# A routed feed-forward kernel: first layer's weights folded, fp16 halves made before the scatter, engine loops unrolled

## The chip, the cores and the metric

One core of one Trainium2 chip runs the whole kernel. The metric is the device time of one execution in microseconds (us). The engines are TensorE (PE), VectorE (DVE), ScalarE (ACT), GpSimd (POOL) and SyncE (SP); each has a queue of its own that runs in order, and they meet in semaphores.

## The reference

The input is x of 16 x 256 rows of 128 numbers (4096 tokens). Two steps are computed, each followed by a LayerNorm of the sum with its input:

1. An attention-like step. Differences of neighbouring rows are normed, compared with 64 guidance vectors (a softmax over dot products), blended with them, and summed over a window of the last eight positions with fixed weights.
2. A feed-forward step with eight experts. Each token goes to the one expert with the largest router probability, and that probability is its gate:

```python
xn = (xt - mu) * rsqrt(var + LN_EPS) * ln_g + ln_b
h = relu(xn @ W1[expert] + b1[expert])      # 128 -> 512
y = (h @ W2[expert] + b2[expert]) * gate    # 512 -> 128
out = layernorm(xt + y)
```

All arrays are float32, and W1 and W2 hold 2 MB each.

## The kernel before, in words

**Windows.** The 4096 tokens are cut into 8 units of 4 tiles of 128. A software pipeline written out in Python runs over turns i; in each turn an engine does the steps of several units. SyncE first issues all loads in one queue: x in pieces, the constants, W1 behind the second piece, the rest of x, then the small ones (Wr, br, ln_g, ln_b; semaphore `small`), W2, and the biases. In turn i VectorE does `window(i)` (mixing of unit i-1, LayerNorm statistics of unit i-2, routing of units i-3 and i-4), `diff(i+2)`, `factors(i)`, in turns 2 to 4 some maxima of W2, and then `directions(i+1)`, which gives the normed rows N; in turns 0 and 1 two maxima of W1 each stand behind that. TensorE does `nT_(i)` (transposes of N), `logits(i-3)`, `sims(i)` (one fp32 matmul of 512 columns), `traj(i-1)`, `rank(i-3)`, `infl(i)`, `xT_(i-2)`. ScalarE copies `nT_`, exponentiates `et`, does `tanh`, `x1` (the first LayerNorm's output), `sumsq`, `xT_` and `np_`, in that order. GpSimd takes the roots (`mag_roots`, `std_roots`) and, in turn i, scatters unit i-4 to DRAM: four indirect DMAs of 128 rows each (L374), each token to the region of its expert, so that afterwards every block of 128 rows belongs to one expert. A row is `ROW = D + 4` floats: x1, the gate's part, the root of the second LayerNorm, and the token number.

**Weights.** For layer matmuls at fp16 speed with nearly fp32 precision, each operand is split in a high and a low fp16 half, and three products are summed. `scales` finds powers of two, `weights_hi` (ScalarE) and `split_lo` (VectorE) make the halves, in turns 7 and later; the last two `split_lo` stand behind the block table. The biases are split in three bf16 parts (`split_bias`), and a matmul with a selector (`sel16`) adds them.

**Blocks.** There are NB = 39 blocks, each of which loads its 128 rows (`XR`), and whose expert is read from a table into registers. Per block: ScalarE scales the rows (`b_xs`, L668), TensorE transposes them in fp32 (L518), ScalarE applies scale and bias per channel (`b_xt`, L673) and makes the high half (`b_xh`, L677), VectorE the low half (`b_xl`, L1000). Layer one is 4 chunks of 4 matmuls (`b_h`: bias L545, then L547, L548, L549). ScalarE makes the relu's high half (`b_hh`, L682), VectorE the low one (`b_hl`, L1006). Layer two (`b_y`) is 4 matmuls of 256 columns (L559: high by both weight halves, into two parts of a PSUM bank), 4 of 128 (L562) and a bias (L561). VectorE adds the two parts to x1 with the gate (`b_z0` L1011, `b_z` L1015), takes statistics, and ScalarE writes `OUT`. GpSimd computes the gate (`token`: cg L398, tok L399) and stores the block by an indirect DMA (`store`, L405). `steps` runs these with fixed leads; the first and last blocks are written out, and between them an engine loop takes eight blocks per turn.

## Time and profile before

| | us |
|---|---|
| Median of 3 runs | 222.06 (220.68 to 222.31) |
| Profiled execution, first to last instruction (span) | 219.4 |
| TensorE busy | 151.0 (69%) |
| VectorE busy | 171.0 (78%) |
| ScalarE busy | 141.9 (65%) |
| GpSimd busy | 122.4 (56%) |

Of the profiled execution only the span is given; a run's time lies 2.7 us above it by the median. Busy time is the sum of an engine's instructions; a matmul counts with its pipeline, so neighbours overlap, and starts tell more than durations. The windows end with the last scatter shortly before 120 us; the blocks take the rest. "Granted clock" is the share of full speed that TensorE was given.

### The profile page before, as it was taken

How to read it: one execution, taken by the hardware profiler on the slowest of the kernel's cores; microseconds unless marked ns; L12 is line 12 of the kernel's file. 1: busy time of each engine (PE TensorE's matmuls, PEld its weight loads, DVE VectorE, ACT ScalarE, POOL GpSimd, SP SyncE). 2: the span in 40 equal slices, each digit the busy share in tenths (PEclk: the TensorE clock that was granted, in tenths of full speed). 3: DMA queues.
4: the chain of work that ended last, by engine and by line, in shares of the span. 5: the costliest groups of instructions: out<-in, count | busy, mean ns of one | idle time of the engine just before them, and what ended most of it. 6: DMA issues, size and time to landing. Idle time of an engine off the chain costs nothing.

```text
span 219.4 us, 5683 instructions
## 1 busy us (share of the span) xinstructions
PE 151.0 (69%) x1395; PEld 125.6 (57%) x1396; DVE 171.0 (78%) x792; ACT 141.9 (65%) x425; POOL 122.4 (56%) x210
## 2 busy tenths in 40 slices
PE   0158975989785989662500199979979979979600
PEld 0014854776664768552400089869869869868500
DVE  2538789878889889986779139989979979989910
ACT  2455619473817386658502288979979979989530
POOL 4322233325728676687777220667767767768670
PEclk9999997585968596655555559999999999999955
DMA  5996760000101010100133211222221221220000
GB/s 154 334 366 190 224 185 0 3 1 0 51 0 38 17 37 14 51 25 25 37 93 106 75 37 28 65 62 56 71 73 52 64 73 54 70 62 23 30 9 0
DMA packets 16409, 15.66 MB, mean 71 GB/s; under 512 B 2810, under 2 KB 13142, under 8 KB 16386
## 3 DMA queue, kind: packets, MB, share of 16 engines
q1 hardware_dynamic: 13458, 10.83, 17.4%
q0 software_dynamic: 2272, 4.27, 5.9%
q10 hardware_dynamic: 656, 0.30, 0.5%
q8 instruction: 9, 0.15, 0.3%
q14 instruction: 14, 0.11, 0.2%
HBM read 10.52 MB, written 5.33 MB: 72 GB/s over the span
## 4 chain that ended last, share of the span: by engine, by line
PE 37%; POOL 18%; issue 13%; DVE 12%; ACT 8%; DMA 5%; DVEq 2%; SPq 1%; ACTq 1%; POOLq 1%
POOL rows L374 12%; PE bank L559 7%; PE bank L545 4%; PE bank L547 4%; PE bank L549 4%; PE bank L548 4%; PE bank L562 3%; PE bank L450 3%; DMA XN<-in_attn_embeddings 3%; PE bank L471 3%; PE bank L518 2%; POOL rstd L362 2%; POOL R L366 2%; ACT sq L578 2%; DVE hl L1006 2%
## 5 line engine op out<-in xcount | busy, mean ns | idle before, releaser
L405 POOL DMA_INDIRECT out<-OUT,tok x39 | 40.5, 1038 | 29.3 <-issue 29.0
L374 POOL DMA_INDIRECT rows<-R,place x32 | 33.9, 1061 | 9.0 <-issue 9.0
L545 PE MATMUL bank<-sel,bias 96*128 (+1 forms) x156 | 35.2, 225 | 5.2 <-issue 5.2
L547 PE MATMUL bank<-xh,W1h 128*128 128x128 f16 x156 | 35.0, 225 | 0.0
L549 PE MATMUL bank<-xh,W1l 128*128 128x128 f16 x156 | 34.8, 223 | 0.0
L548 PE MATMUL bank<-xl,W1h 128*128 128x128 f16 x156 | 34.7, 222 | 0.0
L559 PE MATMUL bank<-W2hl,hh 128*128 x156 | 32.7, 274 | 0.9 <-DVE hl L1006 0.8
L1006 DVE SCALAR_TENSOR_TENSOR hl<-bank,hh 128x512 f16<-128x512 f32 x39 | 26.6, 682 | 6.5 <-ACT hh L682 6.4
L450 PEld LDWEIGHTS bank<-V,C 128*128 128x128 f32 x128 | 24.9, 299 | 11.2 <-issue 11.2
L450 PE MATMUL bank<-V,C 128*128 128x129 f32 x128 | 26.8, 393 | 3.0 <-DVE Y L772 3.0
L562 PE MATMUL bank<-W2hl,hl 128*128 x156 | 28.0, 219 | 0.0
L682 ACT ACTIVATE hh<-bank 128x512 f16<-128x512 f32 x39 | 23.3, 597 | 6.6 <-PE bank L549 6.5
L518 PE MATMUL bank<-C,xs 128*128 128x128 f32 x39 | 11.9, 304 | 14.0 <-ACT xs L668 14.0
L691 ACT ACTIVATE OUT<-z,sd 128x128 f32<-128x128 f32 x39 | 19.4, 499 | 2.5 <-DVE sd L1033 2.5
L668 ACT ACTIVATE xs<-XR 128x128 f32<-128x128 f32 x39 | 15.7, 404 | 7.7 <-DMA XR<-rows 7.6
L362 POOL TENSOR_TENSOR rstd<-var_in,minus_half 128x4 f32<-128x4 f32 x8 | 8.2, 1020 | 20.1 <-DVE var_in L803 20.1
L545 PEld LDWEIGHTS bank<-sel,bias 96*128 96x128 bf16 x156 | 15.5, 99 | 6.4 <-issue 6.0
L559 PEld LDWEIGHTS bank<-W2hl,hh 128*128 128x128 f16 x156 | 15.2, 97 | 5.5 <-issue 2.9
L673 ACT ACTIVATE xt<-bank,gbs 128x128 f32<-128x128 f32 x39 | 17.9, 458 | 0.1
L1000 DVE TENSOR_TENSOR xl<-xt,xh 128x128 f16<-128x128 f32 x39 | 12.4, 318 | 6.0 <-ACT xh L677 6.0
L471 PE MATMUL bank<-nT,gdT 128*64 128x512 f32 x16 | 13.1, 912 | 5.0 <-ACT nT L599 5.0
L547 PEld LDWEIGHTS bank<-xh,W1h 128*128 x156 | 15.7, 100 | 0.6
(162 smaller groups left out, 448.8 us busy)
## 6 DMA issues: line engine op xcount, KB each, us to landing
XR<-rows SPq DMA_DIRECT2D x39, 66.0 KB, 1.8
W<-in_ffn_W SPq DMA_DIRECT2D x1, 2048.0 KB, 11.5
X<-in_attn_embeddings SPq DMA_DIRECT2D x2, 512.0 KB, 9.0
X<-in_attn_embeddings SPq DMA_DIRECT2D x1, 768.0 KB
out<-OUT,tok POOLq DMA_INDIRECT x39, 2.3
XN<-in_attn_embeddings SPq DMA_DIRECT2D x2, 256.0 KB, 8.3
rows<-R,place POOLq DMA_INDIRECT x32, 2.4
C<-in_constants SPq DMA_DIRECT2D x1, 428.0 KB, 4.6
```

Source lines behind the costliest of these rows:

```text
L374: pool.indirect_dma_start(out=rows[:, :], out_offset=bass.IndirectOffsetOnAxis(ap=place[u % 4][:, k:k + 1], axis=0), in_=R[u % 4][:, k, :] ...
L405: pool.indirect_dma_start(out=out[:, :], out_offset=bass.IndirectOffsetOnAxis(ap=tok[k][:, 0:1], axis=0), in_=OUT[k][:, :], in_offset=None ...
L450: m = pe.matmul(tile_of(traj_ps, k), band[a][k % 2], V[u % 3][:, 2 * (k // 2) + a, :], start=a == 0, stop=a == 1)
L471: pe.matmul(sims_ps[0:G, :], gdT[:, :], nT[:, :], start=True, stop=True).then_inc(s["sims_ps"], 1)
L545: pe.matmul(h, bias3[:, c * P:(c + 1) * P], sel, start=True, stop=False)
L547: pe.matmul(h, wh, xh[k][:, :], start=False, stop=False)
L548: pe.matmul(h, wh, xl[k][:, :], start=False, stop=False)
L549: m = pe.matmul(h, wl, xh[k][:, :], start=False, stop=True)
L559: pe.matmul(y[:, 0:2 * D], hh[k][:, c * P:(c + 1) * P], w, start=c == 0, stop=False)
L562: m = pe.matmul(y[:, 0:D], hl[k][:, c * P:(c + 1) * P], W2hl[:, bass.ds(e * FC + c, 1), 0:D], start=False, stop=c == FC - 1)
L682: act.activation(hh[k][:, :], bank[1 + k % 4][:, :], ACT.Relu).then_inc(every["hh"], 1)
L1006: stt(hl[k][:, :], bank[1 + k % 4][:, :], 0.0, hh[k][:, :], ALU.max, ALU.subtract).then_inc(t["hl"][k], 1)
```

## The change

It does the following.

- The second LayerNorm's gain and offset and b1 go into W1. With s = 4 the rows become s (xhat + 1), and since xhat sums to zero, each expert's W1 becomes ln_g W1 + c, with one c per column, (sum of (ln_b - ln_g) W1, plus b1) / 128. TensorE computes c by two fp32 matmuls of 512 columns per expert (`fold`, two experts in each of turns 1 to 4, in banks 0 and 1), with stationaries that VectorE prepares in turn 0 (`stationary`); VectorE applies it (`fold`). The bias matmuls of layer one go. W1's halves wait for the fold.
- The scaled row and its fp16 halves are made in the windows (`xs_`, `xh_` on ScalarE, `rest` on VectorE) and scattered with x1; a row is now 2 D + 8 = 264 floats. In a block two fp16 transposes and one ScalarE copy replace xs, transpose, xt, xh and xl.
- Layer two accumulates all in 128 columns of one bank: 13 matmuls, and one VectorE instruction for z.
- The engine loops are written out; row buffers are 16 rather than 8, and GpSimd scatters the output by the token number in the row buffer, without tok.
- The biases in three parts are b2 only; b1 is loaded by itself behind ln_b.

The diff, cut to its core:

```diff
-ROW = D + 4
+ROW = 2 * D + 8
+X1 = D
+GATE = 2 * D
+TOKEN = 2 * D + 1
+SIGMA = 4.0
 UN = 8
+RN = 16
...
+            sp.dma_start(b1[:, :], b1_in).then_inc(ld["b1"], 16)
             sp.dma_start(W2[:, :, :, :], w2.rearrange("e (c p) d -> p e c d", p=P)).then_inc(ld["w2"], 16)
             sp.wait_ge(s["zeroed"], 1)
             for j in range(3):
-                sp.dma_start(bias[32 * j:32 * j + E, 0:FF], b1).then_inc(ld["bias"], 16)
-                sp.dma_start(bias[32 * j:32 * j + E, FF:FF + D], b2).then_inc(ld["bias"], 16)
...
+                n = j % RN
+                if j >= RN:
+                    sp.wait_ge(every["xT_ps"], j - RN + 1)
+                    sp.wait_ge(every["z"], j - RN + 1)
+                    sp.wait_ge(every["cg"], j - RN + 1)
+                    sp.wait_ge(stored[n], 16 * (j // RN))
+                sp.dma_start(XR[n][:, :], rows[bass.ds(row[k], P), :]).then_inc(row_loaded[n], 16)
+            for n in range(RN):
+                sp.wait_ge(stored[n], 16 * (NB // RN + (n < NB % RN)))
...
                 pool.wait_ge(s["var2_in"], u + 1)
+                if u >= 2:
+                    pool.wait_ge(s["xs"], u - 1)
+                pool.tensor_tensor(r2[u % 2][:, :], var_in[u % 2][:, 1, :], half[:, :], ALU.pow).then_inc(s["r2"], 1)
                 if u >= 4:
                     pool.wait_ge(scattered[u % 4], 16 * NT * (u // 4))
-                pool.tensor_tensor(R[u % 4][:, :, D + 1], var_in[u % 2][:, 1, :], half[:, :], ALU.pow)
-                pool.tensor_copy(R[u % 4][:, :, D + 2].bitcast(I32), C[:, C_TOK + u * NT:C_TOK + (u + 1) * NT]).then_inc(s["r2"], 1)
...
-                pool.wait_ge(s["r2"], u + 1)
+                pool.wait_ge(s["token"], u + 1)
+                pool.wait_ge(s["xl"], u + 1)
                 for k in range(NT):
...
-                pool.nop().then_inc(seen, 1)
-                after(pool, stored[k], count(0) * 16)
-                pool.nop().then_inc(seen, 1)
...
+                    q, k = j + 2, (j + 2) % UN
+                    pool.wait_ge(row_loaded[q % RN], 16 * (q // RN + 1))
+                    if q >= UN:
+                        pool.wait_ge(every["z"], q - UN + 1)
+                    pool.tensor_scalar(cg[k][:, :], XR[q % RN][:, GATE:GATE + 1], scl[:, 3:4], None, ALU.mult).then_inc(every["cg"], 1)
+                if 0 <= j - 2 < NB:
+                    q, k = j - 2, (j - 2) % UN
+                    pool.wait_ge(every["out"], q + 1)
+                    pool.nop().then_inc(seen, 1)
+                    pool.indirect_dma_start(
+                        out=out[:, :], out_offset=bass.IndirectOffsetOnAxis(ap=XR[q % RN][:, TOKEN:TOKEN + 1].bitcast(I32), axis=0),
+                        in_=OUT[k][:, :], in_offset=None, bounds_check=T - 1, oob_is_err=False).then_inc(stored[q % RN], 16)
         @block.tensor
...
+            def fold(q):
+                if q == 0:
+                    pe.wait_ge(s["stationary"], 1)
+                    pe.wait_ge(ld["w1"], 16)
+                for h in range(2):
+                    e = 2 * q + h
+                    pe.matmul(c_ps[h][:, :], Am[:, :], W1[:, e, :], start=True, stop=False)
+                    pe.matmul(c_ps[h][:, :], ident[0:E, e:e + 1].to_broadcast([E, P]), b1[:, :], start=False, stop=True).then_inc(s["c_ps"], 1)
             def rank(u):
...
+                if i - 1 in FOLD_AT:
+                    pe.wait_ge(s["folded"], 2 * FOLD_AT.index(i - 1) + 2)
                 if i < NU:
...
+                if i in FOLD_AT:
+                    fold(FOLD_AT.index(i))
                 if 2 <= i <= NU + 1:
...
+            def b_h(j):
+                k, e = j % UN, expert[j]
+                pe.wait_ge(every["xT"], j + 1)
+                if j >= 4:
+                    pe.wait_ge(every["hl"], j - 3)
                 for c in range(FC):
-                    h = bank[1 + k % 4][:, c * P:(c + 1) * P]
-                    pe.matmul(h, bias3[:, c * P:(c + 1) * P], sel, start=True, stop=False)
+                    h = bank[1 + j % 4][:, c * P:(c + 1) * P]
                     wh, wl = W1h[:, bass.ds(e * FF + c * P, P)], W1l[:, bass.ds(e * FF + c * P, P)]
-                    pe.matmul(h, wh, xh[k][:, :], start=False, stop=False)
-                    pe.matmul(h, wh, xl[k][:, :], start=False, stop=False)
-                    m = pe.matmul(h, wl, xh[k][:, :], start=False, stop=True)
+                    pe.matmul(h, wh, XT[k][:, 0, :], start=True, stop=False)
+                    pe.matmul(h, wh, XT[k][:, 1, :], start=False, stop=False)
+                    m = pe.matmul(h, wl, XT[k][:, 0, :], start=False, stop=True)
...
+            def b_y(j):
+                k, e = j % UN, expert[j]
+                y = bank[5 + j % 2][:, 0:D]
...
+                pe.wait_ge(every["hl"], j + 1)
+                pe.matmul(y, sel16[:, j:j + 1].to_broadcast([96, P]), bias3[:, :], start=True, stop=False)
...
-                        pe.matmul(y[:, 0:D], sel16[:, bass.ds(count(0) * UN + k, 1)].to_broadcast([96, P]), bias3[:, FF:FF + D], start=False, stop=False)
-                    m = pe.matmul(y[:, 0:D], hl[k][:, c * P:(c + 1) * P], W2hl[:, bass.ds(e * FC + c, 1), 0:D], start=False, stop=c == FC - 1)
+                    w = bass.ds(e * FC + c, 1)
+                    pe.matmul(y, hh[k][:, c * P:(c + 1) * P], W2hl[:, w, 0:D], start=False, stop=False)
+                    pe.matmul(y, hh[k][:, c * P:(c + 1) * P], W2hl[:, w, D:2 * D], start=False, stop=False)
+                    m = pe.matmul(y, hl[k][:, c * P:(c + 1) * P], W2hl[:, w, 0:D], start=False, stop=c == FC - 1)
                 m.then_inc(every["y_ps"], 1)
-            steps(pe, [(1, b_h), (4, b_xT), (0, b_y)], load_experts)
+            def b_xT(j):
+                k = j % UN
+                pe.wait_ge(row_loaded[j % RN], 16 * (j // RN + 1))
+                if j >= 2:
+                    pe.wait_ge(every["xT"], j - 1)
+                for h in range(2):
+                    m = pe.transpose(bank[7 * (j % 2)][:, 0:P].bitcast(F16)[:, h * P:(h + 1) * P],
+                                     XR[j % RN][:, h * D // 2:(h + 1) * D // 2].bitcast(F16), id16[:, :])
+                m.then_inc(every["xT_ps"], 1)
+            load_experts(0)
+            for j in range(-4, NB):
+                if 0 < j and j % UN == UN - 2 and j + 2 < NB:
+                    load_experts(j + 2)
+                if 0 <= j + 1 < NB:
+                    b_h(j + 1)
+                if j + 4 < NB:
+                    b_xT(j + 4)
+                if j >= 0:
+                    b_y(j)
...
+            def xs_(u):
+                act.wait_ge(s["x1"], u + 1)
+                act.wait_ge(s["r2"], u + 1)
+                if u >= 1:
+                    act.wait_ge(s["xl"], u)
+                for k in range(NT):
+                    a = act.activation(xs[:, k, :], R[u % 4][:, k, X1:X1 + D], ACT.Identity, scale=r2[u % 2][:, k:k + 1], bias=SIGMA)
+                a.then_inc(s["xs"], 1)
+            def xh_(u):
+                act.wait_ge(s["xs"], u + 1)
+                act.activation(R[u % 4][:, :, 0:D // 2].bitcast(F16), xs[:, :, :], ACT.Identity).then_inc(s["xh"], 1)
             def xT_(u):
                 act.wait_ge(s["xT_ps"], u + 1)
...
                     np_(i + 1)
+                if 2 <= i <= NU + 1:
+                    xs_(i - 2)
+                    xh_(i - 2)
...
+                    act.wait_ge(every["xT_ps"], q + 1)
+                    if q >= UN:
+                        act.wait_ge(every["h_ps"], q - UN + 1)
+                    act.activation(XT[k][:, :, :], bank[7 * (q % 2)][:, 0:P].bitcast(F16).rearrange("p (h t) -> p h t", h=2),
+                                   ACT.Identity).then_inc(every["xT"], 1)
         @block.vector
...
-                    ts(var_in[y % 2][:, 1, :], sy[:, VP, :], LN_EPS, None, ALU.add).then_inc(s["var2_in"], 1)
+                    ts(var_in[y % 2][:, 1, :], sy[:, VP, :], LN_EPS, SIGMA ** -2, ALU.add, ALU.mult).then_inc(s["var2_in"], 1)
...
+            def rest(u):
+                dve.wait_ge(s["xh"], u + 1)
+                tt(R[u % 4][:, :, D // 2:D].bitcast(F16), xs[:, :, :], R[u % 4][:, :, 0:D // 2].bitcast(F16), ALU.subtract).then_inc(s["xl"], 1)
             def directions(u):
...
+            def stationary():
+                dve.wait_ge(ld["small"], 64)
+                dve.wait_ge(ld["b1"], 16)
+                ts(b1[:, :], b1[:, :], 1.0 / D, None, ALU.mult)
+                tt(gbA[:, :], gb[:, 1:2], gb[:, 0:1], ALU.subtract)
+                dve.drain()
+                ts(Am[:, :], ones[:, :], gbA[:, 0:1], 1.0 / D, ALU.mult, ALU.mult).then_inc(s["stationary"], 1)
+            def fold(q):
+                for h in range(2):
+                    e = 2 * q + h
+                    dve.wait_ge(s["c_ps"], e + 1)
+                    stt(W1[:, e, :], W1[:, e, :], gb[:, 0:1], c_ps[h][:, :], ALU.mult, ALU.add).then_inc(s["folded"], 1)
             def split_lo(q):
...
                     guide()
+                if i == 0:
+                    stationary()
...
                     ts(scl[:, 8:12], xT_ps[:, P:P + 4], 2.0 ** -40, None, ALU.max).then_inc(s["max_read"], 1)
+                if 3 <= i <= NU + 2:
+                    rest(i - 3)
+                if i in FOLD_AT:
+                    fold(FOLD_AT.index(i))
                 if 8 <= i <= 9:
...
+                if 0 <= j < NB:
+                    k = j % UN
+                    dve.wait_ge(every["cg"], j + 1)
+                    dve.wait_ge(every["y_ps"], j + 1)
+                    if j >= UN:
+                        dve.wait_ge(every["out"], j - UN + 1)
+                    stt(z[k][:, :], bank[5 + j % 2][:, 0:D], cg[k][:, :], XR[j % RN][:, X1:X1 + D], ALU.mult, ALU.add).then_inc(every["z"], 1)
```

In ScalarE's and VectorE's block loops the remaining instructions are in the order relu, output, root, XT (ScalarE) and hl, aggregate, z, reciprocal, stats, shift (VectorE), with the waits of their buffers.

## Rows read from the trace of the kernel before

**Rows 1.** By stretch: us; busy of PE, PEld, DVE, ACT, POOL; clock; DMA.
```profile
18.68:58.90 40.22, 33.29 (x166) 24.94 (x164) 34.09 (x161) 23.11 (x82) 15.34 (x21) 0.79 0.25 69
58.90:101.14 42.24, 32.40 (x181) 26.71 (x179) 36.87 (x237) 25.52 (x63) 28.33 (x32) 0.70 0.08 28
...
130.00:207.00 77.00, 70.93 (x983) 63.77 (x981) 71.30 (x297) 69.66 (x214) 50.12 (x101) 1.00 0.20 55
```

**Rows 2.** SyncE's issue of ln_b (start, us), and its DMA's us to landing.
```profile
20.91 0.43 SPq L295 DMA_DIRECT2D gb<-in_ffn_ln_b  x1
...
gb<-in_ffn_ln_b SPq DMA_DIRECT2D x1, 0.5 KB, 2.7
```

**Rows 3.** VectorE's timeline, where turns 0, 1, 3, 4, 5 begin.
```profile
13.10 0.16 DVE L842 TENSOR_TENSOR st<-sumsq_in,rmag 128x4 f32<-128x4 f32 x1 [1.72 <-POOL rmag L357]
...
18.68 0.23 DVE L746 RECIPROCAL st<-bank 128x2 f32<-128x2 f32 x2
...
35.13 0.21 DVE L742 TENSOR_SCALAR st<-bank 128x2 f32<-128x2 f32 x2
...
44.61 0.20 DVE L733 TENSOR_REDUCE cnt<-oh 128x8 f32<-128x32 f32 x1
...
58.90 0.19 DVE L733 TENSOR_REDUCE cnt<-oh 128x8 f32<-128x32 f32 x1
```

**Rows 4.** TensorE's timeline: sims, traj and infl, at either clock level.
```profile
27.79 1.07 PE L471 MATMUL bank<-nT,gdT 128*64 128x512 f32 x2 [0.69 <-ACT nT L599]
...
31.44 1.16 PE L423 MATMUL bank<-gdz,ET 64*128 64x129 f32 x8
...
39.04 1.97 PE L471 MATMUL bank<-nT,gdT 128*64 128x512 f32 x2
40.94 3.81 PE L450 MATMUL bank<-V,C 128*128 128x129 f32 x16
```

**Rows 5.** ScalarE's timeline: x1 of a unit, and the copy nT.
```profile
53.86 1.63 ACT L612 ACTIVATE R<-Y,st,rstd 128x128 f32<-128x128 f32 x4
...
59.59 0.57 ACT L599 ACTIVATE nT<-bank 128x512 f32<-128x512 f32 x1
```

**Rows 6.** Timeline: VectorE in turn 7, GpSimd's last root and last scatter.
```profile
78.68 0.24 DVE L746 RECIPROCAL st<-bank 128x2 f32<-128x2 f32 x2 [0.32 <-PE bank L423]
...
101.14 1.04 POOL L362 TENSOR_TENSOR rstd<-var_in,minus_half 128x4 f32<-128x4 f32 x1 [0.65 <-DVE var_in L803]
...
119.11 0.96 POOL L374 DMA_INDIRECT rows<-R,place  x1 [0.30 <-issue]
```

**Rows 7.** VectorE's timeline: hl of three blocks running, a loop turn before the last.
```profile
158.79 0.68 DVE L1006 SCALAR_TENSOR_TENSOR hl<-bank,hh 128x512 f16<-128x512 f32 x1
...
160.68 0.68 DVE L1006 SCALAR_TENSOR_TENSOR hl<-bank,hh 128x512 f16<-128x512 f32 x1
...
163.90 0.69 DVE L1006 SCALAR_TENSOR_TENSOR hl<-bank,hh 128x512 f16<-128x512 f32 x1 [1.26 <-ACT hh L682]
```

**Rows 8.** TensorE's timeline: layer one's first matmul, and the transpose behind layer one.
```profile
149.29 0.22 PE L545 MATMUL bank<-sel,bias 96*128 x1
...
150.20 0.28 PE L518 MATMUL bank<-C,xs 128*128 128x128 f32 x1
```

**Rows 9.** GpSimd's timeline in the blocks: first store, one round, last store.
```profile
137.99 1.05 POOL L405 DMA_INDIRECT out<-OUT,tok  x1 [10.24 <-issue]
...
203.07 1.05 POOL L405 DMA_INDIRECT out<-OUT,tok  x1 [0.30 <-issue]
...
204.17 0.31 POOL L398 TENSOR_SCALAR cg<-XR,scl 128x1 f32<-128x1 f32 x1
...
204.42 0.18 POOL L399 COPY tok<-XR 128x1 int32<-128x1 int32 x1
...
204.92 1.05 POOL L405 DMA_INDIRECT out<-OUT,tok  x1 [0.32 <-POOL tok L399]
...
212.28 0.97 POOL L405 DMA_INDIRECT out<-OUT,tok  x1 [0.30 <-issue]
```

More of the change, by code:

```diff
@@ L78, in constants, with build @@
     return c
-def build(nc, x, guide, wr, br, ln_g, ln_b, w1, b1, w2, b2, cst, rows, out):
+def build(nc, x, guide, wr, br, ln_g, ln_b, w1, b1_in, w2, b2, cst, rows, out):
     with ExitStack() as ctx:
@@ L139, in build @@
         R = [sb(f"R{i}", [P, NT, ROW]) for i in range(4)]
+        r2 = [sb(f"r2{i}", [P, NT]) for i in range(2)]
+        xs = sb("xs", [P, NT, D])
         xT = sb("xT", [P, NT * P])
@@ L182, in build @@
         OUT = [sb(f"OUT{i}", [P, D]) for i in range(UN)]
[L185 removed]
+        ld = {n: sem("ld_" + n) for n in ("cst", "guide", "small", "x0", "x1", "x2", "x3", "w1", "w2", "bias", "b1")}
         names = ("zeroed diff sumsq guarded rmag var_in rstd var2_in r2 mags tanh scales n np nT_ps nT_sb sims_ps ET "
@@ L222, in build @@
         LO_AT = (7, 9)
[L223 to L261 removed]
+        FOLD_AT = (1, 2, 3, 4)
         def pads(eng, first, n):
@@ L309, in _ @@
                 sp.wait_ge(scattered[i], 16 * NT * (NU // 4))
-            held_row = [sp.alloc_register(f"row{i}") for i in range(UN)]
+            held_row = [sp.alloc_register(f"row{i}") for i in range(2 * UN)]
             row = {}
-            def load_rows(first):
-                n = min(UN, NB - first) if isinstance(first, int) else UN
-                sp.load(held_row[0:n], blk_row[0:1, bass.ds(first, n)])
-                for j in range(n):
-                    row[j] = sp.snap(held_row[j], min_val=0, max_val=PADROW)
-            def load(count, k):
-                after(sp, every["z0"], blocks(count(-1), k))
-                after(sp, every["token"], blocks(count(-1), k))
-                sp.dma_start(XR[k][:, :], rows[bass.ds(row[k], P), :]).then_inc(row_loaded[k], 16)
-            steps(sp, [(0, load)], load_rows)
-            for k in range(UN):
-                sp.wait_ge(stored[k], 16 * (NB // UN + (k < NB % UN)))
+            for j in range(NB):
+                k = j % UN
+                if k == 0:
+                    n, half = min(UN, NB - j), (j // UN % 2) * UN
+                    sp.load(held_row[half:half + n], blk_row[0:1, j:j + n])
+                    for i in range(n):
+                        row[i] = sp.snap(held_row[half + i], min_val=0, max_val=PADROW)
+                n = j % RN
[7 more added lines that the diff above has]
+                sp.wait_ge(stored[n], 16 * (NB // RN + (n < NB % RN)))
         @block.gpsimd
@@ L513, in _ @@
             pe.wait_ge(s["split_lo"], 1)
[L515 to L521 removed]
+            held_expert = [pe.alloc_register(f"expert{i}") for i in range(2 * UN)]
             expert = {}
[L524 to L530 removed]
@@ L532, in expert_of, with load_experts @@
-            def expert_of(count, k, lead):
-                if isinstance(count(0), int):
-                    return expert[count(0) * UN + k - expert["first"]]
-                return expert[k if k >= lead else UN + k]
-            def b_h(count, k):
-                e = expert_of(count, k, 1)
-                sel = sel16[:, bass.ds(count(0) * UN + k, 1)].to_broadcast([96, P])
-                pe.wait_ge(t["xl"][k], count(1))
+            def load_experts(j):
+                n, half = min(UN, NB - j), (j // UN % 2) * UN
+                pe.load(held_expert[half:half + n], blk_e[0:1, j:j + n])
+                for i in range(n):
+                    expert[j + i] = pe.snap(held_expert[half + i], min_val=0, max_val=E - 1)
```

240 lines of the change are left out of this document (86 added, 154 removed).

## The prediction

> **What bounds the kernel now.** I read the granted clock and busy time by stretch first, then VectorE's order in time, then the waits and the block loop. The kernel has two stages. In the windows, VectorE is busy 34.1 us of 40.2 and then 36.9 of 42.2, while TensorE's clock is on average at 0.79 and 0.70 of full: it moves between its two levels, 1.2 and 2.4 GHz [rows 1]. In the blocks TensorE, VectorE and ScalarE are all busy 70 to 71 us of 77 at 2.4 GHz [rows 1]: no engine is clearly the bound there, and what counts is each one's own content per block.
>
> In the windows the order on each engine is fixed, so a late instruction shifts all behind it. VectorE starts windows 1, 3, 4 and 5 at 18.68, 35.13, 44.61 and 58.90 [rows 3]. From window 5 on, ScalarE and TensorE are only just ahead of it: in window 7 it waits 0.32 us for the influence matmul [rows 6]. The last windows end in GpSimd's fixed tail: from the rstd of the last unit at 101.14 to the last scatter at 119.11 [rows 6] it hardly pauses, so the blocks start about 21 us after that rstd whenever that is.
>
> **A. The load that VectorE now waits for.** `stationary` stands in VectorE's turn i = 0, ahead of `factors`, which starts at 13.10 now [rows 3]. It waits for the small loads and for b1. SyncE issues ln_b only at 20.91, since its queue is behind X and W1, and that load lands 2.7 us after its issue [rows 2]. b1 is issued next, at some 21.4, and so lands at about 24. With three short instructions and a drain (0.9 us by their kin) `factors` starts at 25.0. Behind it come N and its kin (1.6) and two weight maxima (2.3); window 1 then starts at 29.0 in place of 18.68: **+10.3 us**. Everything behind it on VectorE is late, and nothing on TensorE or ScalarE can run ahead, as both need N and the tanh input from VectorE. This load is new in that place; before, nothing needed it until window 3.
>
> **B. The folds.** In turns 1 to 4 TensorE does four fp32 matmuls of 512 columns behind infl(i), and VectorE waits for both experts' results before directions(i+1), so that they stand in the path. The nearest rows are the sims matmul, 128x512 fp32: 1.97 us at 1.2 GHz, 1.07 at 2.4 [rows 4]. Four behind one another, with the pipe's 0.2 us paid once, are 3.6 us at 2.4 GHz and 7.0 at 1.2. I take 3.6: infl runs in 1.16 us, the fast level, where 5 us of work stood before it [rows 4]. For the matmuls ahead of the fold I take the slow level (sims 1.97, traj 3.8 [rows 4]) wherever TensorE waited long before, since in half of the windows of before it is at that. VectorE's own part is one 512-wide PSUM instruction per expert, 0.68 us like hl [rows 7], and only the last of a turn's two is exposed.
> Turn 1: V is ready 1.7 after the start, traj 3.5, infl 1.2, fold 3.6, last VectorE part 0.7, N 1.0, two maxima 2.3, with a small gap or two: 14.9. Turn 2: V 1.8, traj between 2.1 and 3.8 (3.81 by the ratio of sims' two levels [rows 4]), infl 1.2, fold 3.6, 0.7, 1.0: 10.3 to 12.1; VectorE's own content (9.7 now, plus 1.4 for two fold parts) is 11.0, so 11.0 to 12.1, taken 11.5. Turns 1 and 2 together take 26.4, against 35.13 - 18.68 = 16.45 [rows 3]: **+9.9**.
> **C. The halves made in the windows.** xs_ and xh_ are put between np_ and the next nT_ on ScalarE. Four scaled 128-column activations: 1.63 like x1 [rows 5], and one of 512 columns: 0.57 [rows 5]; they overlap a little, so +2.1 us ahead of each nT, and TensorE's sims waits for nT. So turn 3 is one chain behind the turn 2 fold: xT 0.7, np 1.4, xs and xh 2.1, nT 0.6, sims 2.0, traj 3.7, rank 0.3, infl 1.2, fold 3.6, fold part 0.7, N 1.0 = 17.3, against 44.61 - 35.13 = 9.48: +7.8; at 2.4 GHz throughout it would be +5. Turn 4 is the same chain, 17.3, against 58.90 - 44.61 = 14.3, since VectorE there did 3.6 us of maxima that now lie beside TensorE: **+3.0**. Turns 3 and 4: **+10.8**.
> In turns 5 to 7 the 2.1 us come off a slack of 1.0, then 0, then 0.7 (what infl was ahead of VectorE): +1.1, +2.1, +1.4. In turns 8 and 9 VectorE's own `rest` counts, a 512-wide 0.65 each (hl 0.68 [rows 7] is the upper bound): +1.3. Less 1.0 for the shorter scale steps and the bias pieces, now 128 columns and not 640: **+4.9**.
> The tail on GpSimd keeps its instructions. Its scatters now carry 1056 bytes per row in place of 528. No row shows what that costs: at least nothing, at most each scatter's 0.96 [rows 6] twice, for the twelve of the tail +11.5. I take nothing, as a store of 512 bytes [rows 9] takes as long as a scatter of 528 and the row stays one piece; the row load of 135 KB costs perhaps +0.3 at the start.
>
> **D. The blocks.** Now a block takes 1.89 us, and the turn of the engine loop costs 3.22 - 1.89 = 1.33 more [rows 7]; there are four such, 4.8 together. Content after, by starts:
> TensorE: 16 pairs of load and matmul from 149.29 to 150.20 are 0.057 us each [rows 8]. 12 + 2 + 13 = 27 pairs: 1.53 us. (A 256-wide matmul counts as two of 128, so layer two's 13 are no more than before.)
> Here a rule of the Trainium skill speaks against the change. The page "TensorE: Matmul & The Clock Gate", Back-to-back issue gap, gives about 81 ns for each sustained pair of load and matmul at 128 columns. By it, 27 pairs would be 2.2 us, an estimate, and splitting the 256-wide matmuls would lose; the trace has 57 ns, and the trace decides.
> VectorE: hl, aggregate, one z, reciprocal, stats, shift: 0.60 + 0.09 + 0.27 + 0.11 + 0.21 + 0.12 = 1.40 (1.83 before). ScalarE: relu 0.47, output 0.39, root 0.18 and the fp16 copy, 0.30 to 0.50 by its neighbours in width: 1.34 to 1.54.
> GpSimd: a store at 203.07, cg 1.10 later, tok 0.25 later, the next store 0.50 later: 1.85 [rows 9], as near the bound as the others. Without tok the store follows cg's end by the same 0.3: 1.10 + 0.31 + 0.31 = 1.72, at best 1.85 - 0.25 = 1.60. So **GpSimd becomes the bound**, at 1.72.
> The first store starts at 137.99 and the last at 212.28 [rows 9]: 74.3. After: 34 at 1.72 and four at the tail's 1.28 are 63.6: -10.7. xs, fp32 transpose, xt, xh and xl shrink to two transposes and one copy, about 1.3 us less to the first matmul. **-12.0**; if GpSimd kept up with TensorE (38 x 1.53 = 58.1) it would be -17.5.
>
> **Sum.** 10.3 + 9.9 + 10.8 + 4.9 + 0.3 - 12.0 = +24.2 us. The profiled span is 219.4; the median of the runs shown is 222.06, 2.7 more for what lies around the span. The execution's own total isn't given apart from these, so I add to the median: 246, and shade to **244**, because turns 2 to 4 are costed mostly at the slow clock.
>
> **Rivals.** (1) My forecast, 237 to 251: 0.50. (2) The clock stays high and GpSimd isn't the bound: turns 1 and 2 +8.5, 3 and 4 +5.5, 5 to 9 +3.5, blocks -17.5: +10.6, 233, between 226 and 237. For it: the fold's own work keeps TensorE busy. Against: it waits on ScalarE's xs and xh right behind. 0.24, of which 0.04 lies within 1% of before. (3) The folds run at 1.2 GHz (3.4 more in each of four turns) or scatters cost by bytes: +37, 259. 0.10. (4) The block stage doesn't do what it says: ScalarE's copy or GpSimd's store keeps 1.88 per block and only the loop turns go: -6 rather than -12: 252. 0.07. (5) The skill's 81 ns holds for these pairs: 2.19 us per block rather than 1.72, 39 x 0.47 = 18 more: 264. Each pair in the rows speaks against it: 0.02. (6) Faster: the folds hide entirely. It needs VectorE never to wait in `fold(q)` for c_ps. Then of B and C only VectorE's own instructions stay, 5.4 for the folds and 5.2 for rest, of which its idle time (11 us of the two stretches [rows 1]) can take perhaps 6: +10.3 + 4.6 - 1.0 - 17.5 = -3.6, 218. It decides from window costs behind A of less than 7 us. Against it: infl and fold stand in one queue behind traj. 0.07.
>
> **How the numbers follow.** 1% of 222 is 2.2 us, about what a measurement of this kernel tells from no change. Faster 0.07, same 0.04, slower 0.89. The range of 8 in 10 leaves out most of (3), (5), (6) and half of (4): 229 to 255.
>
> **What would show it.** An idle of about 12 us on VectorE before the b1 scaling, ended by a DMA, near 11 to 24 us. VectorE waits before the four folds ended by the c_ps matmul; window 5 starting near 90 in place of 58.90. ScalarE's xs and xh between np and nT with TensorE idle for nT. In the blocks GpSimd without gaps at 1.6 to 1.72 us a block, TensorE with small gaps, no turn of 3 us. I'd be wrong if b1 landed by 14, if the folds took under 2 us, or if blocks stayed near 1.88.

## The result: slower by a quarter

The changed kernel takes 277.5 us (277.04 to 277.84, 4 runs) against 221.38 for the one before in the same runs (220.68 to 222.31): ratio 1.252, 95% interval 1.246 to 1.258. The direction was as forecast. The time, 244 us with a range of 229 to 255, was not: the cost in the windows came out at 36.9 us for 36.2 forecast, the gain in the blocks turned into a loss. Ratios here and below leave out runs over 1.5% above the fastest of their kernel; that concerns three of the ten runs of run 14 and no other.

The first rows are the page's head (engine, busy us, share of the span).
```profile
span 275.9 us, 5864 instructions
...
PE 193.2 (70%) x1466; PEld 136.0 (49%) x1466; DVE 165.0 (60%) x728; ACT 138.2 (50%) x387; POOL 117.5 (43%) x171
```
The span grew by 56.5 us, and only TensorE's busy time grew much. To place the 56.5, I read one border after another. First the load (VectorE's timeline: start, us, instruction, idle before it and what ended it), and SyncE's issue of it:
```profile
23.81 0.41 DVE L936 TENSOR_SCALAR b<-b 8x512 f32<-8x512 f32 x1 [11.55 <-DMA b<-in_ffn_b]
...
28.18 0.23 DVE L756 RECIPROCAL st<-bank 128x2 f32<-128x2 f32 x2
```
```profile
21.42 0.34 SPq L261 DMA_DIRECT2D b<-in_ffn_b  x1
```
Window 1 starts at 28.18 instead of 18.68 [rows 3]: +9.5. The fold of turn 1 on TensorE, and VectorE waiting for it:
```profile
34.28 1.16 PE L392 MATMUL bank<-gdz,ET 64*128 64x129 f32 x8
35.37 1.12 PE L448 MATMUL bank<-W,Am 128*128 128x512 f32 x2
...
38.53 1.12 PE L449 MATMUL bank<-b,C 8*128 8x512 f32 x2
...
46.68 3.78 PE L419 MATMUL bank<-V,C 128*128 128x129 f32 x16 [1.30 <-DVE Y L782]
```
```profile
37.58 0.75 DVE L946 SCALAR_TENSOR_TENSOR W<-W,gb,bank 128x512 f32<-128x512 f32 x1 [5.83 <-PE bank L449]
...
43.65 0.22 DVE L752 TENSOR_SCALAR st<-bank 128x2 f32<-128x2 f32 x2
...
57.78 0.22 DVE L752 TENSOR_SCALAR st<-bank 128x2 f32<-128x2 f32 x2
...
74.81 0.20 DVE L743 TENSOR_REDUCE cnt<-oh 128x8 f32<-128x32 f32 x1
...
91.27 0.19 DVE L743 TENSOR_REDUCE cnt<-oh 128x8 f32<-128x32 f32 x1
```
The four matmuls ran at the fast clock level, starts 1.05 apart, 4.2 us together. (The last row is turn 2's traj, for later.) Windows 2 to 5 start at 43.65, 57.78, 74.81 and 91.27, where windows 3, 4 and 5 started at 35.13, 44.61 and 58.90 [rows 3]. The end of the windows and the first row load (GpSimd's timeline, then SyncE's):
```profile
137.56 1.04 POOL L330 TENSOR_TENSOR rstd<-var_in,minus_half 128x4 f32<-128x4 f32 x1 [0.59 <-DVE var_in L813]
...
155.88 0.96 POOL L345 DMA_INDIRECT rows<-R,place  x1 [0.30 <-issue]
```
```profile
159.35 5.88 SPq L293 DMA_DIRECT2D XR<-rows  x10
```
That root stood at 101.14, the last scatter at 119.11 [rows 6], and the first row load at 122.43. So the span before the blocks grew by 36.9 us, and the blocks, from the first row load to the end, by the rest: 116.55 us against 96.97, +19.6.

| | forecast | measured |
|---|---|---|
| A. wait for b1 | +10.3 | 28.18 - 18.68: +9.5 |
| B. turns 1 and 2 | +9.9 | (57.78 - 28.18) - 16.45: +13.2 |
| C. turns 3 and 4 | +10.8 | (91.27 - 57.78) - 23.77: +9.7 |
| C. turns 5 to the last root | +4.9 | (137.56 - 91.27) - 42.24: +4.1 |
| last root to the row load | +0.3 | 21.79 - 21.29: +0.5 |
| D. blocks | -12.0 | 116.55 - 96.97: +19.6 |

Inside a block, TensorE's timeline of the changed kernel, in the middle of the block stage:
```profile
200.75 0.23 PE L515 MATMUL bank<-XT,W1h 128*128 128x128 f16 x1 [0.81 <-ACT XT L701]
...
200.87 0.22 PE L517 MATMUL bank<-XT,W1l 128*128 128x128 f16 x1
200.98 0.23 PE L515 MATMUL bank<-XT,W1h 128*128 128x128 f16 x1
...
201.71 0.27 PE L542 MATMUL bank<-id,XR 128*128 128x128 f16 x2
201.83 0.22 PE L527 MATMUL bank<-bias,sel 96*128 96x128 bf16 x1
201.97 0.23 PE L530 MATMUL bank<-W2hl,hh 128*128 x1
202.09 0.23 PE L531 MATMUL bank<-W2hl,hh 128*128 x1
...
202.39 0.23 PE L530 MATMUL bank<-W2hl,hh 128*128 x1
...
202.91 0.23 PE L530 MATMUL bank<-W2hl,hh 128*128 x1
...
203.10 0.22 PE L532 MATMUL bank<-W2hl,hl 128*128 x1
203.26 0.23 PE L515 MATMUL bank<-XT,W1h 128*128 128x128 f16 x1
```
Starts, not durations, are to be read. The three pairs of a layer one chunk should take 0.17 us at 0.057 each [rows 8]; the chunks follow one another by 0.24 ((201.71 - 200.75) / 4). In layer two it is 0.26 and more. Most starts are 0.05 to 0.08 apart. Inside the two layers the longer steps, 0.11 to 0.23, all stand in front of a matmul that takes the expert's weights from an address not used by the one before: each chunk's first in layer one (L515), the second in layer two (L531), and twice the first there (L530: 201.83 to 201.97, and 202.16, not shown, to 202.39). Not every new address shows such a step; L517 follows at 0.06. And TensorE still counts as busy, with everybody waiting for it (waits: us in total, times, longest):
```profile
DVE hl L1034 <- ACT hh L680: 42.8, 39, 6.7
...
ACT hh L680 <- PE bank L517: 23.9, 39, 1.8
```
By the starts of L527 a block takes 2.475 us (mean of 30 between readings of the expert table), against 1.847 before, measured alike.

### The profile page after: what moved, and what is told of

Same layout as the page of the kernel before. It is cut to its first block, busy times and chain, and to the rows that moved or that the text cites. A ratio compares the mean times of both kernels' runs of the same rounds, so it can differ in the third digit from the quotient of the medians.

```text
span 275.9 us, 5864 instructions
## 1 busy us (share of the span) xinstructions
PE 193.2 (70%) x1466; PEld 136.0 (49%) x1466; DVE 165.0 (60%) x728; ACT 138.2 (50%) x387; POOL 117.5 (43%) x171
## 4 chain that ended last, share of the span: by engine, by line
PE 56%; ACT 10%; DVE 9%; SPq 8%; issue 7%; POOL 4%; DMA 3%; DVEq 1%; POOLq 1%; ACTq 1%
PE bank L515 8%; PE bank L419 7%; PE bank L531 7%; PE bank L530 6%; PE bank L517 4%; PE bank L440 3%; PE bank L516 3%; PE bank L448 3%; PE bank L449 3%; PE bank L532 3%; PE bank L392 3%; PE bank L542 2%; POOL rows L345 2%; ACT xs L613 2%; ACT V L582 2%
## 5 line engine op out<-in xcount | busy, mean ns | idle before, releaser
L376 POOL DMA_INDIRECT out<-OUT,XR x39 | 39.7, 1017 | 53.5 <-ACT OUT L687 26.9
L515 PE MATMUL bank<-XT,W1h 128*128 128x128 f16 x156 | 36.0, 232 | 3.8 <-ACT XT L701 3.7
L530 PE MATMUL bank<-W2hl,hh 128*128 x156 | 35.8, 229 | 0.0
L531 PE MATMUL bank<-W2hl,hh 128*128 x156 | 35.7, 229 | 0.1
L516 PE MATMUL bank<-XT,W1h 128*128 128x128 f16 x156 | 34.8, 224 | 0.0
L517 PE MATMUL bank<-XT,W1l 128*128 128x128 f16 x156 | 34.8, 224 | 0.0
L419 PEld LDWEIGHTS bank<-V,C 128*128 128x128 f32 x128 | 24.2, 291 | 11.5 <-issue 9.9
L515 PEld LDWEIGHTS bank<-XT,W1h 128*128 x156 | 15.4, 99 | 14.5 <-issue 5.3
L542 PE MATMUL bank<-id,XR 128*128 128x128 f16 x78 | 11.3, 228 | 13.4 <-DMA XR<-rows 13.3
L694 ACT ACTIVATE sd<-mv,epsc 128x1 f32<-128x1 f32 x39 | 11.5, 294 | 18.0 <-DVE mv L1041 18.0
L410 PE MATMUL bank<-C,N 128*128 128x128 f32 x32 | 7.8, 389 | 15.3 <-DVE N L870 10.9
L530 PEld LDWEIGHTS bank<-W2hl,hh 128*128 128x128 f16 x156 | 15.1, 97 | 6.6 <-issue 0.7
L701 ACT ACTIVATE XT<-bank 128x256 f16<-128x256 f16 x39 | 14.3, 365 | 7.9 <-PE bank L542 7.8
L531 PEld LDWEIGHTS bank<-W2hl,hh 128*128 128x128 f16 x156 | 15.1, 97 | 5.4 <-issue 0.2
```

What stands on the lines that cost most here:

```text
L376: pool.indirect_dma_start(out=out[:, :], out_offset=bass.IndirectOffsetOnAxis(ap=XR[q % RN][:, TOKEN:TOKEN + 1].bitcast(I32), axis=0), in_ ...
L419: m = pe.matmul(tile_of(traj_ps, k), band[a][k % 2], V[u % 3][:, 2 * (k // 2) + a, :], start=a == 0, stop=a == 1)
L515: pe.matmul(h, wh, XT[k][:, 0, :], start=True, stop=False)
L516: pe.matmul(h, wh, XT[k][:, 1, :], start=False, stop=False)
L517: m = pe.matmul(h, wl, XT[k][:, 0, :], start=False, stop=True)
L530: pe.matmul(y, hh[k][:, c * P:(c + 1) * P], W2hl[:, w, 0:D], start=False, stop=False)
```

## Experiments

**1. Fixed experts.**
```diff
-                pe.load(held_expert[half:half + n], blk_e[0:1, j:j + n])
-                    expert[j + i] = pe.snap(held_expert[half + i], min_val=0, max_val=E - 1)
+                    expert[j + i] = (j + i) % E
```

> The changed kernel with the expert of block j fixed to j modulo 8 when the program is written, so no weight address is worked out in a register; it leaves out the routing of a block to its own expert. The matmuls, their shapes and their order are the same. Theory A (TensorE's queue spends about 0.13 us on each fused address operation and 0.10 us on each plain one, and a block of the changed kernel has 12 and 4 of them, so 1.96 of its 2.47 us): the block falls to GpSimd's bound, 1.72 to 1.80 us, and the kernel to 246 to 251 us. Theory B (every instruction of straight-written code costs about 0.033 us whatever it is; 16 of 75 go): the block takes about 1.95 us and the kernel 256 to 259. Theory C (the new order of waits between the engines is the bound): the block stays at 2.4 to 2.5 us and the kernel at 274 to 278.

Measured: 251.99 us (251.88 to 252.1), 1 us above A's range, block 1.90, no pause. At least 25.5 us of the changed kernel's time hang on the addresses and the readings of the experts (both are gone here, and another bound took over). C falls as an explanation of 2.475, B stays possible. The block stood at exactly 1.90 each time, above GpSimd's figure, with TensorE (first row), ScalarE (second) and VectorE (third) all waiting in turn, one timeline each:
```profile
207.11 0.22 PE L526 MATMUL bank<-bias,sel 96*128 96x128 bf16 x1 [0.23 <-DVE hl L1033]
```
```profile
207.09 0.29 ACT L693 ACTIVATE sd<-mv,epsc 128x1 f32<-128x1 f32 x1 [0.47 <-DVE mv L1040]
```
```profile
206.27 0.69 DVE L1033 SCALAR_TENSOR_TENSOR hl<-bank,hh 128x512 f16<-128x512 f32 x1 [0.49 <-ACT hh L679]
```
That is a ring over two in-order queues: mv stands behind hl on VectorE, hh behind sd and XT on ScalarE, sd waits for mv and hl for hh.

**2. Layer two as before (256 columns, z in two steps), all else changed.**
```diff
-                    pe.matmul(y, hh[k][:, c * P:(c + 1) * P], W2hl[:, w, 0:D], start=False, stop=False)
-                    pe.matmul(y, hh[k][:, c * P:(c + 1) * P], W2hl[:, w, D:2 * D], start=False, stop=False)
+                    pe.matmul(y[:, 0:2 * D], hh[k][:, c * P:(c + 1) * P], W2hl[:, bass.ds(e * FC + c, 1), :], start=c == 0, stop=False)
```

> The changed kernel with layer two as it was before: hh by both weight halves in one matmul of 256 columns, z in two steps on VectorE. Each chunk loses one matmul and one fused address operation, the array works as long, VectorE gets 0.35 us more in a block. Theory A: 4 x 0.13 = 0.52 us less in a block, 1.95 to 2.05 us, and 39 blocks give 257 to 261 us. Theory B: 8 instructions of 0.033 less, 2.2 us, 266 to 269. Theory C: no gain or a loss from the longer chain over VectorE, 276 to 285.

Measured: 257.18 us (257.07 to 257.28), block 1.924. A's number, at the lower end of its 257 to 261; B's 266 and C's 276 are out. The array's columns are the same, so the split cost 20.3 us net, though this edit also gives VectorE its second z instruction back.

**3. The kernel before with its loops written out.** `steps` is a Python loop over all blocks.
```diff
-            with eng.Fori(1, turns) as turn:
+            for b in range(-hi, NB - lo):
```

> The kernel before with its engine loops written out and nothing else changed. The prediction credited this with 4.8 us. Theory A: the turns of the loops lose their 1.6 us each, but each reading of eight experts from SBUF still costs TensorE 0.7 to 0.9 us: 1 to 3 us faster, 218 to 221. Theory B (straight-written code is slow in itself): slower, 225 to 245 us.

Measured: 220.25 us (219.24 to 221.33, 8 runs), ratio 0.993 (0.988 to 0.997). Its blocks are as long as before (1.854), so code written out isn't slow in itself: B is out. And the interval between blocks in which a turn begins shrinks from 3.34 to 2.80, not to 1.85: 0.95 of it was never the loop.

**4. One static matmul more in each layer one chunk of the changed kernel.**
```diff
+                    pe.matmul(h, bias3[:, :], sel16[:, j:j + 1].to_broadcast([96, P]), start=True, stop=True)
                     pe.matmul(h, wh, XT[k][:, 0, :], start=True, stop=False)
```

> The changed kernel with one more matmul of 128 x 128 at the head of each chunk of layer one, overwritten by the next one, its addresses fixed: 4 more in a block, no address operation more. Theory A: a chunk takes 4 x 0.057 = 0.23 us of the array against 0.235 of the queue, so they are hidden: block 2.47 to 2.52 us, kernel 277 to 280 us. Theory B: 4 x 0.033 = 0.13 us more in a block, 282 to 284. Were the array the bound, 4 x 0.057 = 0.23 us more in a block, 286 to 288.

Measured: 279.03 us (278.74 to 279.32), block 2.508. 156 matmuls more cost 1.5 us, 0.01 each, though each takes 0.057 of the array. The array idles in every chunk, while the page's busy share says it doesn't.

**5. The kernel before with layer two split in three of four chunks.** The changed kernel's step, put into the old one.
```diff
+                    if c == 0:
                         pe.matmul(y[:, 0:2 * D], hh[k][:, c * P:(c + 1) * P], W2hl[:, w, :], start=True, stop=False)
+                    else:
+                        pe.matmul(y[:, 0:D], hh[k][:, c * P:(c + 1) * P], W2hl[:, w, 0:D], start=False, stop=False)
+                        pe.matmul(y[:, D:2 * D], hh[k][:, c * P:(c + 1) * P], W2hl[:, w, D:2 * D], start=False, stop=False)
```

> The kernel before with layer two's matmul of 256 columns cut into two of 128 in three of its four chunks, to the same two regions of PSUM: as many columns in the array, one fused address operation and one matmul more in each of the three. Theory A (address operations on TensorE's queue): the queue's block goes from 4 x 0.23 + 4 x 0.13 = 1.44 us to 1.83, with about 0.3 us of waits 2.1 to 2.2 against 1.88: 229 to 235 us. If the operations lie beside the matmuls: 221 to 224.

Measured: 233.75 us (233.55 to 233.95), ratio 1.052 (1.048 to 1.057), block 2.068. TensorE's timeline, one chunk of layer two and the start of the next:
```profile
161.87 0.23 PE L562 MATMUL bank<-W2hl,hh 128*128 x1
162.00 0.23 PE L563 MATMUL bank<-W2hl,hh 128*128 x1
162.06 0.22 PE L566 MATMUL bank<-W2hl,hl 128*128 x1
162.13 0.23 PE L562 MATMUL bank<-W2hl,hh 128*128 x1
```
A chunk is 0.26 again (162.13 - 161.87), of which 0.13 stand between the two halves of what was one matmul. The kernel before was so near this edge that three more addresses cost it some 10 of the 11.5 us. The rest, about 1.2 us, is one block of 3.27 us behind a reading of experts, in which the granted clock was 0.51.

**6. The price of b1's place.** Wr, br, g, b and b1 are issued behind the constants, ahead of the 2 MB of W1.
```diff
             sp.dma_start(C[:, :], cst).then_inc(ld["cst"], 16)
+            sp.dma_start(Wr[:, :], wr).then_inc(ld["small"], 16)
...
+            sp.dma_start(b1[:, :], b1_in).then_inc(ld["b1"], 16)
```

> The changed kernel with the small loads and the new load of b1 started right behind the constants, ahead of the 2 MB of W1; nothing else moves. In the prediction the wait for b1 stands for 10.3 us, paid once, in turn 0. If it is a plain delay of everything behind it: 266 to 269 us. If what follows would have waited anyway (W1 lands late, VectorE's maxima): 271 to 277.

Measured: 269.82 us (269.69 to 269.95), 7.7 less. VectorE has b1 in time, and window 1 starts at 20.14, 1.5 us after the old 18.68:
```profile
12.76 0.41 DVE L936 TENSOR_SCALAR b<-b 8x512 f32<-8x512 f32 x1
...
20.14 0.23 DVE L756 RECIPROCAL st<-bank 128x2 f32<-128x2 f32 x2
```

**7. The price of the folds.** No `fold` on TensorE and VectorE; W1 stays as loaded.
```diff
-                if i in FOLD_AT:
-                    fold(FOLD_AT.index(i))
```

> The changed kernel without the folding of W1: the 16 matmuls into c and the 8 updates of W1 on VectorE are left out, so ln_g, ln_b's part and b1 are missing from layer one; the wait for b1 in turn 0 stays. The prediction gave the folds 9.9 us in turns 1 and 2 and most of 10.8 in turns 3 and 4. If the folds cost what they occupy, 4 x (4.2 + 0.6) = 19 us less: 257 to 260. If part of them lies under waits that stay: 262 to 268.

Measured: 255.38 us (255.21 to 255.55), 22.1 less, more than the highest forecast. Row loads start at 136.59 instead of 159.35.

**8. The price of the halves in the windows.** 
```diff
-                    xs_(i - 2)
-                    xh_(i - 2)
...
-                    rest(i - 3)
```

> The changed kernel without the making of the fp16 halves in the router's turns: xs and xh on ScalarE and xl on VectorE are left out, rows are scattered at the same size with zeros in place of the halves, so layer one gets zeros. The prediction gave this 4.9 us in turns 5 to 9 and a part of turns 3 and 4. If so: 268 to 272 us. If ScalarE's share lies beside VectorE's chain: 274 to 277. If more hangs on it than the prediction saw: under 266.

Measured: 272.80 us (272.35 to 273.24), 4.7 less; row loads at 154.76, 4.6 earlier. The prices add: in row loads, 8.1 for b1 (151.27), 22.8 for the folds, 4.6 for the halves are 35.5 of the 36.9 us.

**9. Both repairs.** 2 and 6 together.

> The changed kernel with both repairs together: the small loads and b1 ahead of W1, and layer two's wide matmul. Alone they gave 7.7 us (277.5 to 269.8) and 20.3 us (to 257.2). They lie in different stages, so they should add: 248 to 251 us, still 27 us above the kernel before, of which the folds are most.

Measured: 249.57 us (249.27 to 249.87), ratio 1.124. They add.

**10. The ring, in the same kernel.** bn_aggr of block j-1 goes ahead of hl of block j+1 in VectorE's loop.
```diff
             for j in range(-1, NB + 2):
+                if 0 <= j - 1 < NB:
...
+                    dve.bn_aggr(mv2[k][:, :], bn2[k][:, :]).then_inc(every["mv"], 1)
                 if 0 <= j + 1 < NB:
```

> The same kernel, early b1 and wide layer two, with VectorE's bn_aggr of block j-1 put ahead of hl of block j+1 instead of behind it. With fixed experts the block stood at 1.90 us in every block while TensorE waited 0.23 us for hl and ScalarE 0.47 us for mv: a ring hl, mv, sd, XT, hh, hl over two in-order queues. Theory ring: without the mv link ScalarE starts XT and hh 0.2 to 0.4 us earlier, and the block is left to TensorE's queue, 4 x 0.23 + 4 x 0.13 and waits, 1.75 to 1.85 instead of 1.93: 244 to 247 us. If TensorE's queue alone sets 1.93: as e8, 248 to 251.

Measured: 250.46 us (250.45 to 250.48), block 1.920. No gain: the ring isn't what holds this kernel. VectorE's timeline shows what does. From 168 to 238 us only four of its rows have an idle before them, each at a reading of experts; this is one period (two short rows left out):
```profile
199.87 0.34 DVE L1049 SCALAR_TENSOR_TENSOR zpart<-bank,cg,XR 128x128 f32<-128x128 f32 x1
...
200.24 0.35 DVE L1059 SCALAR_TENSOR_TENSOR z<-bank,cg,zpart 128x128 f32<-128x128 f32 x1
200.63 0.30 DVE L1064 BATCH_NORM_STATS2 bn<-z 128x6 f32<-128x128 f32 x1
...
200.96 0.18 DVE L1034 BATCH_NORM_AGGREGATE mv<-bn 128x2 f32<-128x6 f32 x1
201.15 0.69 DVE L1041 SCALAR_TENSOR_TENSOR hl<-bank,hh 128x512 f16<-128x512 f32 x1
201.75 0.34 DVE L1049 SCALAR_TENSOR_TENSOR zpart<-bank,cg,XR 128x128 f32<-128x128 f32 x1
```
1.88 us: with z in two steps VectorE is full, as it nearly was before the change. The expectation named TensorE's queue as the rival's reason; the trace names VectorE.

**11. The ring, with fixed experts.** The same move in the kernel of 1.

> The kernel with fixed experts, which leaves out the routing of a block to its own expert, with bn_aggr of block j-1 ahead of hl of block j+1. Without address operations only the ring or a busy engine is left as a bound of 1.90 us. Theory ring: the block falls to 1.55 to 1.75 us, the kernel from 252.0 to 240 to 246. If 1.90 is the array's or GpSimd's own time: 251 to 253.

Measured: 240.72 us (240.70 to 240.74), 11.3 less than 1; block 1.531. The ring was real, and without ring and addresses the block is the array's time: TensorE's matmuls start 0.05 to 0.06 us apart nearly throughout. Busy time by stretch (us; busy and count of PE, PEld, DVE, ACT, POOL; clock; DMA), here and in the changed kernel:
```profile
180.00:200.00 20.00, 20.00 (x357) 19.85 (x355) 19.49 (x80) 18.70 (x53) 17.29 (x27) 1.00 0.44 119
```
```profile
180.00:200.00 20.00, 19.80 (x216) 14.54 (x216) 11.71 (x46) 11.77 (x30) 10.30 (x16) 1.00 0.29 78
```
Both call TensorE busy all the time, one with 357 matmuls in 20 us, one with 216. At 0.056 us each the latter fill 12.1 us. VectorE, at 19.49 of 20, is nearly full too. GpSimd keeps up as well, without tok, at 1.54 a block (its timeline):
```profile
199.87 1.02 POOL L376 DMA_INDIRECT out<-OUT,XR  x1 [0.17 <-issue]
200.94 0.30 POOL L370 TENSOR_SCALAR cg<-XR,scl 128x1 f32<-128x1 f32 x1
201.41 1.02 POOL L376 DMA_INDIRECT out<-OUT,XR  x1 [0.17 <-issue]
```

**12 and 13. One layer fixed, the other dynamic,** with bn_aggr first: in `b_h` alone, then in `b_y` alone,
```diff
-                k, e = j % UN, expert[j]
+                k, e = j % UN, j % E
```

> The changed kernel with bn_aggr first on VectorE and the expert fixed to j modulo 8 in layer one alone; it leaves out layer one's routing. Left are layer two's 8 fused address operations, 8 x 0.13 = 1.04 us of the 1.96. Theory sum (the time of address operations adds to that of the array wherever the queue has not run ahead): 1.53 with fixed experts and 2.47 with both layers dynamic, so about half of the 0.94 goes: 1.9 to 2.1 us in a block, kernel 257 to 264 us with the experts still read. Theory hidden (the queue runs ahead in layer one's chunks): 1.6 to 1.75, kernel 245 to 250.

> The same with the expert fixed in layer two alone; it leaves out layer two's routing. Left are layer one's 4 fused and 4 plain operations, 0.92 us of the 1.96. Theory sum: 1.9 to 2.1 us in a block, a little under the kernel with layer one fixed, 255 to 263 us. Theory hidden: 1.55 to 1.7, kernel 243 to 249.

Measured: layer one fixed 251.89 us (251.69 to 252.09), block about 1.78 (readings left out); layer two fixed 242.16 us (242.13 to 242.19), block 1.53. The sum theory fails in both. Layer one's 4 fused and 4 plain operations alone cost nothing per block, layer two's 8 fused alone 0.25, both together 0.94 (2.475 - 1.53; the 2.475 has bn_aggr in its old place, and no run has it first with both layers dynamic and the split). So the address work doesn't simply add to the array's time. It fits that TensorE's queue runs ahead and does it beside matmuls, until there is more of it than the matmuls last; that is argued, and how far ahead it can run wasn't measured.

**14. The kernel before, loops written out, experts read twice (21 and 19) instead of five times.**
```diff
-            held_expert = [pe.alloc_register(f"expert{i}") for i in range(UN + AHEAD)]
+            held_expert = [pe.alloc_register(f"expert{i}") for i in range(20 + AHEAD)]
```

> The kernel before with its loops written out, as e3, and the experts read on TensorE in two readings of 21 and 19 instead of five of up to 9. e3's block was 1.88 us and 2.7 to 2.9 at four readings. Theory: a pause is mostly the fixed time of a reading, and three of the four go: 3 x 0.9 = 2.7 us less than e3's 220.25, with a longer pause at block 20: 217 to 219 us. If the pause goes by the number of registers: the remaining one is twice as long and 219 to 221 us comes out.

Measured: 219.63 us (217.57 to 221.4, 10 runs), ratio 0.988 (0.984 to 0.992, seven runs); 3 is not told apart from it. Starts of layer two's bias matmul around the one reading left (L552), with the first matmuls behind the reading (L536), and the stretch behind it in the form of run 11:
```profile
164.12 0.22 PE L552 MATMUL bank<-bias,sel 96*128 96x128 bf16 x1
...
166.01 0.22 PE L552 MATMUL bank<-bias,sel 96*128 96x128 bf16 x1
...
168.88 0.29 PE L536 MATMUL bank<-sel,bias 96*128 96x128 bf16 x1 [2.09 <-issue]
...
169.31 0.31 PE L536 MATMUL bank<-sel,bias 96*128 96x128 bf16 x1
...
171.02 0.31 PE L552 MATMUL bank<-bias,sel 96*128 96x128 bf16 x1
```
```profile
168.88:171.02 2.14, 2.14 (x19) 1.99 (x20) 0.00 (x0) 0.13 (x1) 0.67 (x3) 0.50 0.23 56
```
The interval is 5.01 us, 3.1 more than a block, but not all of it is reading. The reading of 19 registers parts two matmul starts by 2.31 us, where 0.06 is usual: some 2.2 us, against 0.8 to 1.0 for readings of 7 or 9 in 3 (starts 0.88 to 1.07 apart). Behind it the granted clock was 0.50, the lower level, and layer one's matmuls start 0.107 us apart ((169.31 - 168.88) / 4), not 0.057; the next interval too is 2.29 long, at a mean of 0.76. Over both intervals 5.01 + 2.29 - 2 x 1.88 = 3.5 us are lost, 2.2 to the reading and 1.3 to the clock. Four readings in 3 cost 4 x 0.95 = 3.8 us at the full clock. So a reading goes roughly by its registers (0.12 and 0.10 us each), and nothing much was saved. 3 and 14 are the only versions here faster than the kernel before, by about 1%, under the 2% that count as a difference here; no version with the changed row format beat it.

## Why the prediction was wrong

**What held.** A, C and the tail were right to within 1.1 us each, with their mechanisms: the wait of 11.55 us for b1 behind SyncE's queue, xs and xh between np and nT, twice the bytes in a scatter at no price (a last root to row load 0.5 us longer). The wait for b1 is worth 8, not 10.3, when removed, since of the delay 1.5 us stay in run 6.

**B was 3.3 us low,** most in turn 2: 14.1 us against 11.5 taken. Four fp32 matmuls at 3.6 us took 4.2: the working took 0.2 us of each as overlap with the next, and their starts are 1.05 apart at 1.12 long, so it is 0.07. And traj of turn 2 started at 46.68, 3.0 us into the turn, where I had 1.8: it waits for VectorE's Y, which reads the bank that traj overwrites. It then took 3.78 us, the upper end of what I had allowed. Run 7 gives all the folds' price as 22 us, more than their own 4 x (4.2 + 0.75) = 20: nearly nothing of them was hidden, so rival 6, the hiding folds, was far off. C's 1.1 us the other way made up part of it, and by luck: its folds were as much too short, but traj of turn 4 ran in 2.59 us, partly at the fast level, where 3.7 was taken.

**D failed, by 31.6 us,** 25.5 of them (run 1) in the term of TensorE. "12 + 2 + 13 = 27 pairs: 1.53 us", with the aside that a matmul of 256 columns counts as two of 128, was right for the array: run 11 measures 1.531. It was wrong as TensorE's time per block, 2.475. I counted columns and pairs and left out what the queue does between them, 12 fused and 4 plain address operations, by the estimate above 1.96 us. They didn't show in the rows I used, since there 16 pairs in 0.91 us [rows 8] are one more pair per chunk, 0.228, about as long as that chunk's addresses, 0.23 to 0.24. Two edits took this balance away: the bias matmuls of layer one went, and its chunk stayed at 0.24 instead of falling to 0.17, and layer two got four more addresses. The second weighs most: run 2 prices it at 20.3 us, beside the 20.8 by which the 38 block intervals grew (96.5 - 75.8), and by run 13 layer one's addresses alone cost nothing.

**"GpSimd becomes the bound, at 1.72"** fails too. Its 0.32 us before a store was a wait for tok [rows 9], not a fixed cost; without tok it is 0.17 and the round 1.54. Behind TensorE's queue stood another bound that I didn't look for, the ring at 1.90 (runs 1 and 11). Had addresses and readings cost nothing, the blocks would have been at 1.90 and the time at 252: the other 6.1 us of D's miss, about 38 x (1.90 - 1.72).

**The loop turns' 4.8 us** (which the sum didn't use; its own 1.33 us a turn would make 5.3) were less than half right: 4 x (3.34 - 2.80) = 2.1 us by the intervals, 1.65 by the medians of run 3. The rest is the reading of experts into registers, which the changed kernel still does: its pauses are 3.45 - 2.475 = 0.97.

**The rivals.** Number 4 was the nearest in kind (the block stage does not do what it says), with 0.07 and a price far too low, since it took 1.88 per block as the worst. Number 5, 264 us, took the Trainium skill's 81 ns per pair ("TensorE: Matmul & The Clock Gate", Back-to-back issue gap). The pairs of run 11 take 57 ns (1.531 / 27), so its reason is out; but its conclusion, that splitting the wide matmuls loses, was right, for another reason. The Trainium skill's "Perfetto Trace Analysis" (Per-instruction lifecycle) says that a matmul's end in the profile is estimated and not observed. No run here shows how the end is made; what the trace of the changed kernel shows is that 216 matmuls, each given as 0.22 us or more, cover 19.8 of 20 us though the array needs 12.1.

## What to carry to other kernels

Count TensorE's instructions with register addresses apart from its matmuls: a matmul split in two for a neater accumulation can double the address work while the array does the same, and the pairs around it are its only cover. Judge TensorE by matmuls started per microsecond, not by busy time. And before an engine is called the next bound, remove the first one in thought and walk each pair of in-order queues for a ring: here two further bounds, 1.90 and 1.88, lay under 2.475. A load that gets its first early user must move up in its queue with it.
